# Second attention with one product by ones for two key chunks, their exponentials added on GpSimd, and queries centered through the weights

## What is computed

```python
q = _ln((x @ Wq + bq).reshape(b, s1, 16, 32), qn_w, qn_b)      # mean and variance over 32 columns
kv = concat([y_main @ Wk + bk, y_main @ Wv + bv]); k = _ln(kv[..., :32], kn_w, kn_b); v = kv[..., 32:]
ctx = softmax(q k^T * 32 ** -0.5) v                             # 496 keys
ctx_dca = softmax(q k_dca^T * 32 ** -0.5) v_dca                 # 16 further keys, a softmax of their own
out = (ctx + ctx_dca) @ Wo + bo
x = x + tanh(g_xattn[1]) * out
```

## Time and profile before

| | us |
|---|---|
| three runs | 2105.7, 2103.86, 2099.7 |
| median | 2103.86 |
| profiled execution | 2100.42 |
| its span in the profile | 2098.7 |

### The profile page before, as it was taken

The page is one execution under the profiler, slowest core; times in us unless marked ns, Lnnn a source line. Parts: engine busy times, 40 slices in busy tenths (PEclk is TensorE's granted clock), DMA queues, the critical chain, the costliest instruction groups (busy, mean ns, idle before and its releaser), DMA issues. The chain is left out here.

```text
span 2098.7 us, 29513 instructions
## 1 busy us (share of the span) xinstructions
PE 2010.1 (96%) x11805; PEld 1598.3 (76%) x11805; DVE 985.4 (47%) x1606; ACT 744.5 (35%) x1167; POOL 669.6 (32%) x657
## 2 busy tenths in 40 slices
PE   6998999999999999999999999999999999899994
PEld 4775687788888888888888888666666658799994
DVE  6776333212122131221312255786777656767755
ACT  5464512112112121121212222555656563455540
POOL 5444301010111101111111057264544141454425
PEclk9998999999999999999999999999999999999997
DMA  5232200103021030010100004533443500588847
GB/s 193 76 131 91 66 1 25 41 1 121 21 101 41 1 121 20 21 40 1 45 16 21 25 1 110 145 82 91 92 97 82 141 22 21 208 274 287 269 164 223
DMA packets 94328, 184.94 MB, mean 88 GB/s; under 512 B 9632, under 2 KB 34720, under 8 KB 91232
## 3 DMA queue, kind: packets, MB, share of 16 engines
q1 hardware_dynamic: 84640, 126.42, 20.2%
q0 software_dynamic: 9552, 56.63, 8.2%
HBM read 141.47 MB, written 54.13 MB: 93 GB/s over the span
## 5 line engine op out<-in xcount | busy, mean ns | idle before, releaser
L1570 POOL TENSOR_TENSOR ML<-MT,MH 128x512 fp32r<-128x512 f32 x128 | 164.9, 1292 | 791.5 <-ACT MH L1372 791.3
L1514 DVE SCALAR_TENSOR_TENSOR X<-PS,WT,X 128x512 f32<-128x512 f32 x128 | 96.0, 750 | 391.1 <-PE PS L57 390.6
L1372 ACT ACTIVATE MH<-MT 128x512 fp32r<-128x512 f32 x128 | 80.9, 632 | 512.4 <-DVE MT L1441 512.4
L55 PE MATMUL PS<-HH,Wg0h 128*128 128x512 f32 x512 | 201.0, 393 | 0.1
L56 PE MATMUL PS<-HL,Wg0h 128*128 128x512 f32 x512 | 200.2, 391 | 0.0
L57 PE MATMUL PS<-HH,Wg0l 128*128 128x512 f32 x512 | 200.2, 391 | 0.0
L55 PE MATMUL PS<-Wd0h,MH 128*128 128x512 f32 x512 | 199.6, 390 | 0.1
L55 PE MATMUL PS<-HH,Wu0h 128*128 128x512 f32 x512 | 199.5, 390 | 0.0
L57 PE MATMUL PS<-HH,Wu0l 128*128 128x512 f32 x512 | 199.3, 389 | 0.0
L56 PE MATMUL PS<-HL,Wu0h 128*128 128x512 f32 x512 | 199.3, 389 | 0.0
L56 PE MATMUL PS<-Wd0l,MH 128*128 128x512 f32 x512 | 199.3, 389 | 0.0
(11 more groups left out here) (477 smaller groups left out, 4337.3 us busy)
## 6 DMA issues: line engine op xcount, KB each, us to landing
HH<-Kd SPq DMA_DIRECT2D x48, 256.0 KB, 4.2
HL<-Qd SPq DMA_DIRECT2D x48, 256.0 KB, 6.3
Od<-OB SPq DMA_DIRECT2D x46, 256.0 KB
STG<-in_Wg SPq DMA_DIRECT2D x8, 1024.0 KB, 5.2
STG<-in_Wu SPq DMA_DIRECT2D x8, 1024.0 KB, 5.3
STG<-in_Wd SPq DMA_DIRECT2D x8, 1024.0 KB, 5.5
X<-in_x SPq DMA_DIRECT2D x16, 256.0 KB, 8.2
Vd<-VO SPq DMA_DIRECT2D x16, 256.0 KB, 2.0
```

Of the source, the lines that this page charges most:

```text
L55: e.matmul(out_, a_[0], b_[0], start=start, stop=False)
L1372: e.activation(M[0][:, f, :], MT[i % 2][:, :], ACT.Copy).then_inc(m_h, 1)
L1514: e.scalar_tensor_tensor(X[:, k, :], PS[:, bank["d", 4 * n + q], :], WT[:, k, x:x + 1], X[:, k, :], ALU.mult, ALU.add).then_inc(d_x, 1)
L1570: e.tensor_tensor(M[1][:, f, :], MT[i % 2][:, :], M[0][:, f, :].bitcast(f32), ALU.subtract).then_inc(m_l, 1)
```

## The change

- Products by ones: `mix` leaves out the groups by ones in chunks 0 and 1. GpSimd adds the exponentials of these two chunks (`add_two`, 1024 columns, into `SUMS`), and chunk 3 has a group by ones for the sum. In chunk 2 TensorE now waits for the sums' bank (`c_b`, before in chunk 0), in chunk 3 for `sum_01`.
- `PT` becomes a ring of four, so the exponential of chunk `u` waits for the products of chunk `u - 4`, and in chunks 0 and 1 for GpSimd's sum. The context becomes a ring of five head groups (`CX`).
- GpSimd's order: `add_two` at `u % 4 == 1`, then `context_sum` (before at `u % 4 == 0`). `context_high` and `context_low` move from `u % 4 == 2` to 3. `q_low` and `q_scale` come one chunk later on GpSimd. The additions of the output bias to X stand one at a time at `u % 32` = 19, 23, 27, 31 (before four at 24).
- Queries: `Wq` and `bq` are centered over each head's 32 columns on VectorE (`q_weights_center`) ahead of their split; `q_means` and `q_center` go, and the square is taken right behind the bias.
- Projections stand at other chunks (`PROJECT_AT`); projection 12 stands behind the first turn after the last chunk.
- The shared expert's first weights are loaded to three free places (`RAW_FRONT`), and GpSimd's constants of the second mixture, all but the first, wait for the last projection.

```diff
-    sb("under_W", [P, 8192])
+    sb("under_W", [P, 5120])
+    PTC, SUMS = sb("PTC", [P, 2, 1024]), sb("SUMS", [P, 1024])
@@ queries
+    def q_weights_center(e):
+        means = RW0[:, 512:592]
+        e.wait_ge(ld_wq, 32)
+        centered = ((STG0[0][:, :], slice(0, 64)), (bq[:, :], slice(64, 80)))
+        for i, (x, at) in enumerate(centered):
+            e.tensor_reduce(means[:, at], heads(x), axis=X_, op=ALU.add).then_inc(wq_mean, 1)
+        e.wait_ge(wq_mean, 2)
+        e.tensor_scalar(means, means, -1.0 / 32, None, ALU.mult).then_inc(wq_mean, 1)
+        e.wait_ge(wq_mean, 3)
+        for x, at in centered:
+            e.tensor_tensor(heads(x), heads(x), means[:, at].unsqueeze(2).to_broadcast([P, at.stop - at.start, 32]),
+                            ALU.add).then_inc(wq_mean, 1)
@@ first mixture, act and dve
-                    e.wait_ge(ld_wq, 32)
+                    e.wait_ge(wq_mean, 5)
...
+                    q_weights_center(e)
                     e.wait_ge(wq_h, 1)
@@ side_jobs
+        PROJECT_AT = {1: (1, 7, 9, 15), 2: (1, 3, 7, 9), 3: (1, 3, 5, 9)}
-            if b and 8 * g + k in (1, 6, 9, 10):
-                jobs.append(("o", 4 * (b - 1) + (1, 6, 9, 10).index(8 * g + k)))
-            if u == NU - 1:
-                jobs.append(("o", 12))
+            if b and 8 * g + k in PROJECT_AT[b]:
+                jobs.append(("o", 4 * (b - 1) + PROJECT_AT[b].index(8 * g + k)))
@@ mix
             e.wait_ge(t_exp, 2 * u + 2)
-            parts = [(ABANK, 0, V[s % 3][:, c, :], c == 0), (BBANK, 0, None, c == 0)]
-            if c == 3:
-                parts += [(ABANK, 256, V[s % 3][:, 4, :], True), (BBANK, 256, None, True)]
...
+            v, x = V[s % 3], PT[u % 4]
+            last = quarters(e, ABANK, 0, v[:, c, :], x, c == 0, c == 3)
+            if c == 2:
+                if w:
+                    e.wait_ge(c_b, 3 * w - 2)
...
+                last = quarters(e, BBANK, 0, ONE[:, 0, :], x, True, False)
+            elif c == 3:
+                quarters(e, ABANK, 256, v[:, 4, :], x, True, True)
+                quarters(e, BBANK, 0, ONE[:, 1, :], x, False, False)
+                e.wait_ge(*sum_01(w + 1))
+                quarters(e, BBANK, 0, ONE[:, 0, :], PT[4], False, True)
+                last = quarters(e, BBANK, 256, ONE[:, 2, :], x, True, True)
             last.then_inc(c_mm, 1)
@@ exponential
-            if u >= 2:
-                e.wait_ge(c_mm, u - 1)
+            if u >= 4:
+                e.wait_ge(c_mm, u - 3)
+                if u % 4 < 2:
+                    e.wait_ge(*sum_01(u // 4))
+            elif u >= 2:
+                e.wait_ge(moe0["d_mm"], 128)
@@ act
-                if u >= 6 and (u - 6) % 4 == 0:
-                    context_high(e, (u - 6) // 4)
+                if u >= 7 and u % 4 == 3:
+                    context_high(e, u // 4 - 1)
@@ GpSimd
+        def add_two(e, w):
+            e.wait_ge(t_exp, 8 * w + 4)
+            if w:
+                e.wait_ge(c_mm, 4 * w)
+            e.tensor_tensor(SUMS[:, :], PTS[0], PTS[1], ALU.add).then_inc(sum_01.sem, 1)
...
-                if u and u % 4 == 0 and u <= NU:
-                    context_sum(e, u // 4 - 1)
-                for t in jobs_of(u - 1, "qq"):
-                    q_center(e, t)
+                if u % 4 == 1:
+                    if u < NU:
+                        add_two(e, u // 4)
+                    if u > 4:
+                        context_sum(e, u // 4 - 1)
@@ second mixture, GpSimd
             e.iota(IO[:, :], pattern=[[1, P]], base=0, channel_multiplier=0).then_inc(made_c.sem, 1)
+            e.wait_ge(a2["o_mm"], 16)
             e.iota(IPU[:, :], pattern=[[0, 1]], base=0, channel_multiplier=1).then_inc(made_c.sem, 1)
```

More of the change, by code:

```diff
@@ L828, in flamingo @@
     QY = sb("QY", [P, 512])
-    TH, TL = sb("TH", [P, 512], f32r), sb("TL", [P, 512], f32r)
+    under_t = ExitStack()
+    TBR = tensors(under_t)("TBR", [P, 1024])
+    under_t.close()
+    TB = sb("TB", [P, 2, 512], f32r)
+    TH, TL = TB[:, 0, :], TB[:, 1, :]
     bq = sb("bq1", [P, 512])
@@ L1708, in second_attention @@
         QS = [slot(HL, i + 1)[0:112] for i in range(3)]
-        Wo, CXS = WU, (M0, WD)
-        PT = [PTB[:, i, :].rearrange("p (h q) -> p h q", h=4) for i in range(2)]
+        Wo = WU
+        CX = [tuple(x[:, i + j, :] for j in range(2)) for x in M0 for i in (0, 2)] + [(WD[0][:, 0, :], WD[0][:, 1, :])]
+        PTS = [x[:, i, :] for x in (PTB, PTC) for i in range(2)]
+        PT = [x.rearrange("p (h q) -> p h q", h=4) for x in (*PTS, SUMS[:, :])]
         vflat = VB
@@ L1770, in second_attention @@
             turns += side_jobs(u)
-        turns += [("o", t) for t in range(13, 16)]
+        turns += [("o", t) for t in range(12, 16)]
         side = {x: 6 + i % 2 for i, x in enumerate(turns)}
@@ L1867, in o_product @@
             for c in range(4):
-                last = mm3(e, PS[:, side["o", t], :], both(CXS[b % 2], ALL, c, slice(n * P, (n + 1) * P)), both(Wo, ALL, c),
+                last = mm3(e, PS[:, side["o", t], :], both(CX[(4 * b + c) % 5], ALL, slice(n * P, (n + 1) * P)), both(Wo, ALL, c),
                            c == 0, c == 3)
@@ L1924, in mix, with quarters @@
             e.wait_ge(t_exp, 2 * u + 2)
-            parts = [(ABANK, 0, V[s % 3][:, c, :], c == 0), (BBANK, 0, None, c == 0)]
-            if c == 3:
-                parts += [(ABANK, 256, V[s % 3][:, 4, :], True), (BBANK, 256, None, True)]
-            for bank, at, w, start in parts:
-                for h in range(4):
-                    if w is None:
-                        w_ = ONE[:, 0 if c < 3 else 1 if at == 0 else 2, :]
-                    else:
-                        w_ = w[:, 32 * h:32 * h + 32]
-                    last = e.matmul(PS[32 * h:32 * h + 32, bank, at:at + 256], w_, PT[u % 2][:, h, :], start=start,
-                                    stop=c == 3, tile_position=(0, 32 * h))
-            last.then_inc(c_mm, 1)
+            v, x = V[s % 3], PT[u % 4]
[3 more added lines that the diff above has]
+                    e.wait_ge(c_b, 3 * w - 2)
+                else:
+                    e.wait_ge(made_one, 3)
+                    q_left[0](e, BBANK)
+                last = quarters(e, BBANK, 0, ONE[:, 0, :], x, True, False)
[5 more added lines that the diff above has]
+                last = quarters(e, BBANK, 256, ONE[:, 2, :], x, True, True)
+            last.then_inc(c_mm, 1)
+        def quarters(e, bank, at, w, x, start, stop):
+            for h in range(4):
+                w_ = w if w.shape[1] == 32 else w[:, 32 * h:32 * h + 32]
+                last = e.matmul(PS[32 * h:32 * h + 32, bank, at:at + 256], w_, x[:, h, :], start=start, stop=stop,
+                                tile_position=(0, 32 * h))
+            return last
         def side_job(e, kind, i):
@@ L1966, in pe @@
             four_front["turn"](e, 0)
-            side_job(e, "o", 13)
+            for t in (12, 13):
+                side_job(e, "o", t)
             four_front["gate"](e)
@@ L2213, in pool @@
                     h_factors(e, STATS_AT[u - 1] // 4)
-                if u < NU and u % 32 == 24:
+                if u < NU and u % 32 in (19, 23, 27, 31):
+                    t = u // 32 * 4 + u % 32 // 4 - 4
                     e.wait_ge(bt_d, 1)
-                    for t in range(u // 32 * 4, u // 32 * 4 + 4):
-                        e.wait_ge(xn, t + 1)
-                        e.tensor_tensor(X[:, t, :], X[:, t, :], bt[:, :], ALU.add).then_inc(x_bt, 1)
+                    e.wait_ge(xn, t + 1)
+                    e.tensor_tensor(X[:, t, :], X[:, t, :], bt[:, :], ALU.add).then_inc(x_bt, 1)
         a2.update(c_mm=c_mm, o_mm=o_mm, t_mm=t_mm, s_max=s_max, maxed=maxed)
@@ L2351, in raw_free, with raw @@
                 e.wait_ge(*w_l(3 * (j - 1)))
+        RAW_FRONT = {"g": WOB[:, 2:4, :].rearrange("p a b -> p (a b)"), "u": STG0[0][:, 1024:2048], "d": TBR[:, :]}
+        def raw(j, which):
+            return part(RAW[j % 2], which) if j else RAW_FRONT[which]
         def load_shared(e, j):
@@ L2355, in load_shared @@
             for which in "gud":
-                e.dma_start(part(RAW[j % 2], which),
+                e.dma_start(raw(j, which),
                             a["s" + which].rearrange("(p c) f -> p (c f)", p=P)).then_inc(ld_ws.sem, 16)
@@ L2364, in shared_front @@
             e.wait_ge(a2["o_mm"], 12)
+            e.wait_ge(q_mm, 16)
+            e.wait_ge(*stored(15))
             load_shared(e, 0)
@@ L2507, in weight_high @@
                 e.wait_ge(*USED[which]((2 if which == "d" else 1) * (i + 1)))
-            e.activation(by_halves(W[j % 2][0][which], which), unsorted(part(RAW[j % 2], which), which), ACT.Copy).then_inc(w_h.sem, 1)
+            e.activation(by_halves(W[j % 2][0][which], which), unsorted(raw(j, which), which), ACT.Copy).then_inc(w_h.sem, 1)
         def tile_high(e, i):
@@ L2653, in weight_low @@
             hi, lo = (x[which] for x in W[j % 2])
```

(2 more changed lines are left out.)

78 lines of the change are left out of this document (26 added, 52 removed).

## The result

The changed kernel takes 2115.1 us (median of four runs, 2113.3 to 2115.9) against 2101.8 us (2099.6 to 2105.7) for the kernel before on the same chip: a ratio of 1.0062, 95% interval 1.0045 to 1.0079. It is slower by some 13 us, where 3.9 us less were forecast, and it lies above the predicted range.

What follows compares the result with a forecast made beforehand. TensorE was taken to bound the kernel, with VectorE's score loop close behind. Ones products -5.7 and port +1.8, all else 0, gave -3.9 us, from 2103.9 to 2100.0 us; the range was 2090 to 2109.

Steps and rivals of the forecast that it cites:

- Ones products: Second attention's chunks: one group by ones fewer per window, chunks 0 and 1 shorter, chunk 3 longer; -5.7 us in all.
- side jobs in both places: Six stretches with side jobs ahead of chunk 0's products and behind chunk 1, covering VectorE; -0.45 us each, -2.7 us.
- Rival 2: VectorE's score loop needs 2.14 instead of 2.02 us and takes back the shortened chunks' gain; +8.1 us, 2112.0; chance 0.10.
- Port: In 8 windows VectorE's small operation in a query tile's variance is delayed beside GpSimd's division; +1.8 us, bounds 0 to 3.6.
- The two new waits of TensorE: Waits for the sums' transpose in chunk 2 and GpSimd's sum in chunk 3, between quarter products; 0, at most 7.7 us.
- The sum's length: GpSimd's new addition of 1024 columns takes 2.4 us, with 1.5 us to spare before anything waits; 0 cost.
- Centering: Centering query weights on VectorE costs it 6.2 us, inside idle time ahead of a subtraction; 0 effect.
- Rings: PT ring of four, CX ring of five: exponentials freed early enough, projections merely come at other chunks; 0 effect.
- Rival 3: GpSimd's sum takes 4.2 us, so ScalarE's copies hold up exponentials; 9.6 us lost, 2107.8; chance 0.08.
- Rival 1: TensorE alone sets the pace in the attention, each window gives its 0.44; -13.6 us, 2090.2; chance 0.18.
- Tail: End of attention: projection 12's former 0.42 us wait takes chunk 3's extra 0.43; GpSimd's constants fit; 0, at worst 1 us.

Runs made afterwards that it cites:

- old_ones_2: Second run of the changed kernel with the earlier kernel's groups by ones in every chunk and no GpSimd sum; ratio 0.9984 to the kernel before.
- ones_and_sum: Changed kernel with the earlier groups by ones, GpSimd's sum still made and waited for by the exponentials but read by no product; ratio 1.0035 to the kernel before.
- drop_01: Changed kernel without GpSimd's sum and without the group by ones that reads it; ratio 0.9968 to the kernel before.
- extra_3: Changed kernel with the earlier groups by ones, no GpSimd sum, and one more group by ones in every chunk 3; ratio 1.0053 to the kernel before.
- narrow_add: Changed kernel with GpSimd's sum cut to 4 of 1024 columns from the second window on; 2112.2 us, ratio 1.0056 to the kernel before.
- center_only: Kernel before with the centering by weights and nothing else; ratio 1.0003 to the kernel before.
- old_ones: Changed kernel with the earlier kernel's groups by ones in every chunk and no GpSimd sum; 2096.2 us, ratio 0.9979 to the kernel before.

## Why the prediction was wrong, by its steps

By groups of four chunks, in us, each from its first turned scores to the next group's:

| from chunk | old_ones_2 | ones_and_sum | after |
|---|---|---|---|
| 4 | 11.96 | 12.85 | 14.64 |
| 8 | 12.68 | 12.84 | 13.73 |
| 84 | 11.72 | 13.10 | 14.91 |
| 92 | 11.72 | 13.10 | 14.92 |
| the other 28 together | 354.1 | 355.9 | 358.8 |

The first four are those of the changed kernel with the lower clock in them. From ones_and_sum to the changed kernel the other 28 grow by 2.9 us, and the four by 6.3. The two kernels differ only in where the groups by ones stand, so the 2.9 is the trade of groups between chunks. Three of the four (from 4, 84 and 92) are of the kind that grows by 0.37 to 0.42 where nothing disturbs it, so some 1.1 of the 6.3 is the trade too. That gives four parts for the attention's 13.6 us: the sum and what it delays +5.7 (ones_and_sum less old_ones_2); the trade +4.0; the lower clock, with the longer waits ahead of it, +5.2; and the rest of the change -1.3 (old_ones_2 less before). The +4.0 agrees with drop_01 and extra_3 (+4.0 at least). The parts are estimates where they overlap: narrow_add, read with half of the lower clock taken off, would give the sum 3.7 us only and the trade 4.3. The forecast had -3.9: 1.8 for the port, -5.7 for the trade, 0 and 0. The miss of 17.5 us is 3.9 + 9.7 + 5.2 - 1.3.

*Ones products, -5.7 forecast, about +4.0 measured.* This is the largest term, and it failed in one step: "chunk 0 gives its 0.44 (3.71 - 0.44 = 3.27, just above VectorE's 3.24)". That compares the pair of scores only with VectorE's transposes at the window's end. The pair also waits for the maxima of the pair ahead of it, one round of the same loop that I had for chunk 1. It comes 3.56 us after the end (1502.70; the turn of the maxima, behind the last group, starts at 1499.14), not 3.27: chunk 0 gives 0.13 to 0.15. I had counted the loop once in a window and it runs twice. Its size was short as well: 2.02 is the round of a pair that has not waited. One that has waited takes 2.12 us, so chunk 1 gives 0.02, and the pair after it is 0.10 late. -0.13 - 0.02 + 0.10 + 0.43 = +0.38, not -0.15. Among the 28 groups, compared with ones_and_sum, there are 11 of these at +0.37 to +0.42, 5 at -0.34 to -0.43 (my "side jobs in both places", 6 at -0.45), the last one at +0.44 with the tail in it, and 11 at about 0. Chunk 3's +0.43 was right (extra_3: 0.44 a group).

*Rival 2* named this mechanism and its threshold ("from 0.12 us more in each round of that loop"; it was 0.10 more). I gave it 0.10 because the reductions themselves last 1.25 to 1.29 us with GpSimd busy or not the earlier trace rows. They do last that in the changed kernel too. But the loop has three terms, and the one that grew was the 0.67 from a pair's start to its reduction. The trace of before had the 0.77: the pair at 1510.27 had waited, and its maxima start at 1511.04:

```profile
1511.04 1.19 DVE L2063 TENSOR_REDUCE VB<-PS 128x2 f32<-128x992 f32 x1 [0.23 <-PE PS L1889]
```

Rival 2's 2112.0 is near the measured time, but by its own sum it holds 25 x 0.43, and the runs split the loss in another way: the loop explains about +4.0, not +8.1. That its total came out near is luck.

*Port, +1.8 forecast (0 to 3.6), +5.7 measured for the sum in all, of which 3.7 in the groups with the long collisions.* The mechanism was right and the place was wrong. I priced the small operation of the variance (L1004), which took 0.64 us once in the attention and 0.17 else. The costly ones were the long operations with two SBUF operands that stand ahead of the maxima: the centering of hidden tiles (1.12 to 2.48 us, twice) and the low part of Wo (1.57 to 2.47, once). I had the earlier trace rows, which show just such a pair, and looked only for where the old GpSimd work would meet VectorE's queries, not for where the new sum of 2.4 us would meet anything.

*The lower clock* has no term in the prediction. Nothing in the trace of before shows it in the attention, and no rival had it; but that trace has it on both sides of the attention, and a change that makes TensorE wait behind shorter work should have had one.

*The two new waits of TensorE, 0 forecast:* right. The three groups stand 0.43 apart (1508.51, 1508.94, 1509.37), and TensorE waits for no sum. *The sum's length, 2.4 us:* right, 2.38 (the context's sum behind it ends at 5.1 + 2.0 = 7.1, not 7.2, which changes nothing). *Centering, 0:* right (center_only, 1.0003). *Rings, 0:* the attention of old_ones, which has them, is shorter than that of before. *Rival 3* (GpSimd late) was not tried by itself. It shows at the end of ones_and_sum (1.1 us); TensorE's waits for exponentials came to 3.3 us in all (2.4 and 0.9), against 1.1 before. *Rival 1* falls with drop_01, whose groups are worth 0.16 and not 0.43.

*Tail, 0 forecast:* from the last chunk's scores to the gate it is 11.47 us instead of 10.65. "Chunk 3's extra 0.43 takes that" was too kind: TensorE waits 0.37 us for exponentials and 0.41 for the context's low part.

```profile
1736.02 1.07 PE L1951 MATMUL PS<-PTC,VB 128*32 128x256 f32 x16 [0.37 <-ACT PTC L1999]
...
1739.82 0.47 PE L55 MATMUL PS<-Wu0h,ML 128*128 128x512 f32 x1 [0.41 <-POOL MH L2211]
```

With the groups left in place (old_ones_2) the same new order of the tail gains 0.7 us.

## What to carry to other kernels

When work is moved from one step of a loop to another, check each step against every loop that it is in, not the first wait behind the move alone; and measure a loop's round on an iteration that has itself waited, since that one is the longer (here 2.12 and not 2.02 us, and the difference took nearly all that chunk 1 was to give). An operation moved to GpSimd must be laid over VectorE's timeline row by row: what counts is the long VectorE operation with two SBUF operands that stands ahead of something TensorE waits for. And where the shorter work leaves TensorE waiting, its clock can fall behind the wait: for such a change, read the granted clock stretch by stretch after the run, and leave room for it in the range.

## What the runs showed of the hardware

- In the attention the granted clock fell to 0.50 beside or behind waits of TensorE of 0.55 to 2.5 us, for 3.4, 6.8 or 10.2 us at a time, and only in the seven kernels with the shorter chunks; a wait of 2.04 us in a kernel with full chunks left it at 1.00.
- A VectorE operation with two SBUF operands of 512 columns (L1670) went from 1.12 to 2.48 us when it started 0.75 us behind a GpSimd sum of 2.38 us; VectorE's reductions of one SBUF operand (675 ns on average with the sum, 676 without, in eight of them) and those out of PSUM (1.29 us) did not change.
- A GpSimd addition of two fp32 operands in SBUF takes 2.38 us for 1024 columns.
- A pair of products that had to wait starts what depends on it 0.10 us later than one that did not (0.77 instead of 0.67 us).
